# A token's two expert rows scattered to places of their own and summed by the next reader, with the padding written beside the last pass

## The chip, the core and the metric

The kernel runs on one core of a Trainium2 chip. The metric is the device time of one execution in microseconds; the median of several runs counts, and a profile shows one execution instruction by instruction. The core's engines work beside each other and meet at semaphores: TensorE (PE) multiplies and transposes, VectorE (DVE) and ScalarE (ACT) work elementwise, GpSimd (POOL) does small vector work and issues the indirect DMAs, SyncE (SP) issues most other DMAs in order. Sixteen DMA engines move the data.

## The reference

The input x holds 32 sequences of 256 tokens, 8192 rows of 128 float32 numbers. Four blocks follow each other, each on a layer norm of x:

```python
x = x + attention_a(layernorm(x))     # 16 heads of 8, softmax over the 256 tokens of a sequence, relative bias
x = x + ffn(layernorm(x))
x = x + attention_b(layernorm(x))     # the same token of all 32 sequences attends to each other
x = x + ffn(layernorm(x))

def ffn(x):                           # shared expert on every token, two of seven routed experts by a router
    out = expert(x, sg, su, sd)
    scores, idx = top_k(softmax(x @ wr.T + rb), 2)      # scores are then divided by their sum
    w = sum(scores[..., None] * one_hot(idx, 7), -2)
    for e in range(7):
        out = out + w[..., e:e + 1] * expert(x, rg[e], ru[e], rd[e])
    return out
# expert(h, g, u, d) = (silu(h @ g.T) * (h @ u.T)) @ d.T, inner width 352
```

## The kernel before

Half A computes attention A and the feed-forward behind it, half B does the same with attention B. Each half has two stages.

The passes. 16 passes of 512 tokens (4 tiles of 128 partitions) run as a software pipeline: the head of pass p+1 (load, norm, projections), the attention of pass p and the tail of pass p-1 (second norm, router, shared expert) are interleaved. The order of the steps on each engine is fixed ahead of time by a planner (`order`) from a table of costs (`WORK`) and of dependences (`needs_head`, `needs_attention`, `needs_tail`). The tail gives every token its rank in the list of each of its two experts (`rank`, VectorE, with the running counts in `taken`) and sends its normed row twice, to the two experts' regions of the DRAM tensor `sent`, by 8 indirect scatters of 128 rows (`scat`, L839, GpSimd). A row in `sent` is 130 words: 128 values, the routing share and the token's row number. The tail also stores x with attention and shared expert added: to `x2` in half A (L679), to `x3` in half B (L682). In half B the head loads x2 by four DMAs a pass (L653); GpSimd adds the output bias to a copy (`keep`, L812) and computes the roots of the norms (L790 to L800).

The expert stage (`blocks`). When all ranks are known, VectorE makes a table of 38 blocks of 512 rows (`make_table`, L1227): which expert, and which rows of `sent`. SyncE writes padding rows behind the end of each expert's list (`pad`, L684), fetches per block the weights (L708, L710, 3 buffers) and the rows (L698, 6 buffers), in the order weights of block b+3, rows of block b+6. The fetch of rows waits until the block six before has been added. TensorE turns the rows (L1324), makes gate and up products in three tiles (L1451 to L1453), the down product (L1526) and transposes back (L1536). VectorE weights the result with the share (`weigh`, L1278). GpSimd adds the 512 result rows into x2 or x3 by four indirect DMAs with addition (L850). Two rows of one token may lie in two blocks, so each block first waits for the adds of all blocks before it (L848):

```python
pool.wait_ge(emptied["T1"], use("E", b, "back"))
after(pool, added, 64 * b)
for t in range(TOK):
    pool.indirect_dma_start(out=dst[:, :], ..., in_=yo[:, b % 2, t, :], in_offset=None, compute_op=ALU.add)
```

Between the halves GpSimd clears the operand buffers `kw` (L858) and `vw` (L860 to L863) of attention B. At the end SyncE copies x3 to the output in four DMAs (L740).

## Time and profile before

| | us |
|---|---|
| median of 3 runs | 2653.86 (2653.19 to 2663.66) |
| the profiled execution | 2653.52 |
| its span from first to last instruction | 2651.7 |
| busy: TensorE, VectorE, ScalarE, GpSimd | 2083.7, 1596.5, 1165.9, 975.9 |
| passes of half A, about | 0 to 1130 |
| expert blocks of half A, about | 1151 to 1544 |
| passes of half B, about | 1562 to 2230 |
| expert blocks of half B, about | 2246 to 2637 |

A profile line names an engine, a line of the kernel and an operation, with tensors as output<-input. The chain of work that ended last is followed back from the last instruction: at each step to what released it. A share of busy time is an average over stages with different limits; what a change in one stage is worth is read in that stage. "issue" is time in which an engine waited for nothing that the profile shows, and SPq, POOLq stand for an engine's queue of DMA-issuing instructions. Landing is the time until a DMA's data has arrived and its semaphore tells so.

### The profile page before, as it was taken

Reading aid. Unit: us, or ns where it says so; the run is one execution under the profiler, and the core shown is the slowest. Engines: PE = TensorE matmul, PEld = TensorE weight load, DVE = VectorE, ACT = ScalarE, POOL = GpSimd, SP = SyncE. Lnnn points to the kernel's source line nnn. Section 1 sums busy time; section 2 is a strip of 40 time slices with the busy share of each in tenths; the row PEclk is TensorE's granted clock in tenths of the full one; section 3 lists DMA queues with packets and bytes.
Section 4 is the critical chain, followed back from the end, with each engine's and each line's share of the span. In section 5 each row is a group of like instructions: output and inputs, shape, how many; then the busy total and the mean of one; then the engine's idle time right before and its main releaser. Section 6 shows DMA issues by size and latency. Waiting matters only on the chain.

```text
span 2651.7 us, 42166 instructions
## 1 busy us (share of the span) xinstructions
PE 2083.7 (79%) x13346; PEld 1340.6 (51%) x13346; DVE 1596.5 (60%) x5677; ACT 1165.9 (44%) x2413; POOL 975.9 (37%) x1113
## 2 busy tenths in 40 slices
PE   6979797979898989858878737777777774988873
PEld 4646464656555555545555414544544443555552
DVE  4758585857676666745555426666666653655542
ACT  4949494849585858522223212322222231333321
POOL 1131414140312121326665653323343322566654
PEclk8979798979888888979999969888888886999986
DMA  5021212121111111066676511111110114566664
GB/s 169 18 77 61 77 61 77 56 83 46 59 47 55 50 49 45 23 144 149 149 153 137 122 24 33 31 29 39 37 37 25 31 28 118 128 153 152 150 141 107
DMA packets 193947, 210.31 MB, mean 79 GB/s; under 512 B 20944, under 2 KB 159440, under 8 KB 193664
## 3 DMA queue, kind: packets, MB, share of 16 engines
q1 hardware_dynamic: 139520, 161.09, 20.2%
q0 software_dynamic: 54208, 46.53, 10.6%
q8 instruction: 110, 1.80, 0.3%
q14 instruction: 109, 0.89, 0.1%
HBM read 114.03 MB, written 59.95 MB: 66 GB/s over the span
## 4 chain that ended last, share of the span: by engine, by line
PE 35%; POOL 19%; DVE 14%; DMA 11%; issue 11%; ACT 4%; another core or an unknown queue 4%; SPq 1%; POOLq 0%; DVEq 0%; ACTq 0%
POOL x L850 13%; DMA x<-arena 10%; PE bank_T L1387 8%; PE bank_S L1377 5%; PE bank_O L1400 4%; PE bank_E L1451 2%; PE bank_Y L1489 2%; DVE arena L1084 2%; DVE z L1097 2%; PE bank_E L1342 2%; POOL rs L792 2%; ACT z L914 2%; PE bank_E L1452 2%; PE bank_E L1453 2%
## 5 line engine op out<-in xcount | busy, mean ns | idle before, releaser
L850 POOL DMA_INDIRECT x<-arena x304 | 470.7, 1548 | 354.0 <-DMA x<-arena 179.6
L1097 DVE CUSTOM_DVE_ANT_0 z<-bank_S,arena 128x256 f32<-128x256 f32 x1024 | 377.6, 420 | 143.0 <-PE bank_S L1377 105.7
L839 POOL DMA_INDIRECT sent<-xs,target x256 | 253.5, 990 | 568.0 <-DVE target L1205 501.6
L914 ACT ACTIVATE z<-z,nm 128x256 f32<-128x256 f32 x1024 | 437.5, 500 | 29.8 <-DVE nm L1097 27.8
L922 ACT ACTIVATE probT<-bank_T 128x512 f32<-128x512 f32 x512 | 284.5, 588 | 120.9 <-remote 64.9
L1387 PE MATMUL bank_T<-cst,z 128*128 128x128 f32 x2048 | 320.7, 292 | 19.8 <-ACT probT L922 9.6
L1387 PEld LDWEIGHTS bank_T<-cst,z 128*128 128x128 f32 x2048 | 237.4, 148 | 112.8 <-issue 49.9
L790 POOL TENSOR_SCALAR rs<-moments 128x4 f32<-128x4 f32 x64 | 16.8, 262 | 675.6 <-DVE moments L1039 673.5
L1377 PE MATMUL bank_S<-arena_r 32*128 32x256 f32 x1024 | 202.3, 342 | 24.3 <-DVE nm L1097 23.3
L1377 PEld LDWEIGHTS bank_S<-arena_r 32*128 32x128 f32 x1024 | 122.5, 194 | 108.5 <-issue 70.4
L976 ACT ACTIVATE arena<-bank_E 128x512 f32<-128x512 f32 (+1 forms) x114 | 68.1, 598 | 193.4 <-PE bank_E L1453 190.0
L1400 PE MATMUL bank_O<-probT,arena 128*32 128x256 f32 x2048 | 148.8, 411 | 3.6 <-issue 2.5
L1265 DVE SCALAR_TENSOR_TENSOR arena<-arena,bank_E 128x512 f32<-128x512 f32 (+1 forms) x114 | 78.2, 686 | 120.8 <-ACT arena L976 117.0
L976 ACT ACTIVATE arena<-bank_S 128x512 f32<-128x512 f32 (+1 forms) x114 | 68.1, 597 | 185.9 <-PE bank_S L1453 177.6
L1451 PE MATMUL bank_E<-arena_r 128*128 128x512 f32 (+1 forms) x228 | 105.3, 462 | 55.7 <-issue 52.8
L1265 DVE SCALAR_TENSOR_TENSOR arena<-arena,bank_S 128x512 f32<-128x512 f32 (+1 forms) x114 | 78.2, 686 | 112.5 <-ACT arena L976 109.1
L1451 PE MATMUL bank_S<-arena_r 128*128 128x512 f32 (+1 forms) x228 | 104.3, 457 | 48.6 <-issue 48.6
L956 ACT ACTIVATE th<-bank_E 128x512 f32<-128x512 f32 (+1 forms) x96 | 57.0, 594 | 176.4 <-PE bank_E L1453 169.0
L1451 PE MATMUL bank_E<-xh,shared_hi 128*128 128x512 f32 (+1 forms) x192 | 99.4, 518 | 34.1 <-DVE th L1210 21.4
L1526 PE MATMUL bank_O<-arena 128*128 128x512 f32 (+1 forms) x228 | 121.9, 617 | 5.0 <-DVE arena L1275 5.0
L966 ACT ACTIVATE arena_r<-bank_T 128x512 fp32r<-128x512 f32 x76 | 45.5, 599 | 182.3 <-PE bank_T L1324 177.1
L1526 PE MATMUL bank_Y<-arena 128*128 128x512 f32 (+1 forms) x228 | 121.7, 616 | 0.0
(172 smaller groups left out, 4120.9 us busy)
## 6 DMA issues: line engine op xcount, KB each, us to landing
arena_r<-w_split SPq DMA_DIRECT2D x76, 704.0 KB
arena_r<-arena SPq DMA_DIRECT2D x128, 256.0 KB, 2.4
arena<-sent SPq DMA_DIRECT2D x76, 260.0 KB
arena<-in_wdp SPq DMA_DIRECT2D x76, 192.0 KB
x<-arena POOLq DMA_INDIRECT x304
xin<-in_x SPq DMA_DIRECT2D x16, 256.0 KB, 3.8
h<-in_x SPq DMA_DIRECT2D x16, 256.0 KB, 3.1
sent<-xs,target POOLq DMA_INDIRECT x256
```

What stands on the lines that cost most here:

```text
L839: pool.indirect_dma_start(out=sent[:, :], out_offset=bass.IndirectOffsetOnAxis(ap=target[:, s, k, t:t + 1].bitcast(U32), axis=0), in_=xs[: ...
L850: pool.indirect_dma_start(out=dst[:, :], out_offset=bass.IndirectOffsetOnAxis(ap=xr[:, b % ROW_RING, t, D + 1:RW].bitcast(U32), axis=0), i ...
L914: last = act.activation(zt, zt, ACT.Exp, bias=nm[:, u % NM_RING, t:t + 1], scale=-1.0)
L922: act.activation(probT[:, u % PT_RING, :], bank[f"T{n % 2}"][:, :], ACT.Copy).then_inc(emptied[f"T{n % 2}"], 1)
L976: act.activation(eth[0:size, k % 2, :], bank[e][0:size, :], ACT.Tanh, scale=0.5).then_inc(eth_ready, 1)
L1097: last = dve.tensor_tensor_reduce(z[:, u % Z_RING, t * SEQ:(t + 1) * SEQ], bank[s][:, t * SEQ:(t + 1) * SEQ], bias_a[:, h, P - P * t:P - P ...
L1265: dve.scalar_tensor_tensor(out=a, in0=a, scalar=1.0, in1=bank[e][0:size, :], op0=ALU.add, op1=ALU.mult).then_inc(emptied[e], 1)
L1377: last = pe.matmul(bank[name][:, t * SEQ:(t + 1) * SEQ], qx[own, s, 0, g, lo:lo + P].bitcast(F32R), qx[own, s, 1, g, b * SEQ:(b + 1) * SEQ ...
L1387: last = pe.transpose(bank[name][:, c:c + P], z[:, u % Z_RING, t * SEQ + k * P:t * SEQ + (k + 1) * P], ident)
L1400: last = pe.matmul(bank["O"][32 * j:32 * j + 32, 0:SEQ], vx[:, p % 2, 2 * b + k, c:c + 32], probT[:, u % PT_RING, k * SEQ:(k + 1) * SEQ], ...
L1451: pe.matmul(dst, high_w, high_x, start=True, stop=False)
L1526: last = pe.matmul(bank[y][:, :], w_d[0:size, b % WEIGHT_RING, i, :], ehid[0:size, b % 2, i, :], start=i == 0, stop=i == NT - 1)
```

## The change

The adds into x2 and x3 become plain scatters. Each token's two result rows go to places of their own in a new DRAM tensor `added_rows` of the half: the first at the token's row number, the second 8192 rows further. Padding rows carry numbers of their own behind those (13 tiles of 512). The wait for earlier blocks on GpSimd goes; the counter `added` is split in two by the block's parity (`wait_added`).

The next reader sums. In half B a pass loads, beside its x2 rows, the two sets of expert rows into `ya` (12 DMAs in place of 4), and GpSimd adds both into `xin` (step `join`) before the norm and `keep` read it. At the end x3 has been loaded to on-chip buffers (`pieces`) by eight DMAs issued among blocks 4 to 11 of half B; SyncE and ScalarE load the two sets of rows (`shares`, eight DMAs each), VectorE adds both to the pieces (`last_sums`) and SyncE stores each piece to the output.

The padding goes out earlier. After the rank of pass 14 VectorE copies `taken` to `ends` (step `pads`), and SyncE writes two chunks of padding rows from DRAM behind the end of each expert's list (14 DMAs); the scatters of the last pass wait for them. The padding tiles are made on GpSimd in passes 7 to 13 of half A. `make_table` loses its last cast and, in half B, its wait for the adds.

Between the halves `kw` is cleared once the last up product of the blocks is done, and `vw` is cleared on VectorE (`clear_values`). The planner's tables get the steps `join` and `pads` and a dearer `load`. Cut to its core:

```diff
 }
+WORK["A"]["pads"] = {"dve": 0.25, "sync": 6.5}
 WORK["B"] = {k: v for k, v in WORK["A"].items() if k not in ("cut", "scores", "probs", "mix", "context", "flip")} | {
-    "keep": {"pool": 1.3}, "turn1": {"pe": 0.6, "act": 2.06}, "v": {"pe": 1.0, "dve": 1.18}, "spr": {"sync": 10.7},
+    "load": {"sync": 5.4}, "join": {"pool": 2.7}, "keep": {"pool": 1.3}, "turn1": {"pe": 0.6, "act": 2.06}, "v": {"pe": 1.0, "dve": 1.18}, "spr": {"sync": 10.7},
     "scores": {"pe": 1.1, "dve": 1.3, "act": 0.6}, "probs": {"pe": 0.5, "act": 0.5},
...
     flip = z[:, 5, 0:P]
-    raw = sb("raw", [P, 2 * INNER])
-    raw_hi = sb("raw_hi", [P, 2 * INNER], F32R)
-    raw_lo = sb("raw_lo", [P, 2 * INNER], F32R)
+    spare = sb("spare", [P, 6 * INNER])
+    raw, raw_hi, raw_lo = (spare[:, 2 * INNER * k:2 * INNER * (k + 1)] for k in range(3))
...
+    ya = spare[:, 0:4 * CHUNK].rearrange("p (s k t d) -> p s k t d", s=2, k=2, t=TOK)
...
+    pieces = [z[:, 2 * c:2 * c + 2, :] for c in range(3)] + [probT[:, 2 * c:2 * c + 2, :] for c in range(4)] + [hid[:, 0:2, :]]
+    shares = [arena_r[:, 0:8192].rearrange("p (c r) -> p c r", c=8), arena[:, 0:8192].rearrange("p (c r) -> p c r", c=8)]
...
+    added_rows = [nc.dram_tensor(f"added_{k}", [2 * ROWS + (ROUTED + IDLE) * CHUNK, D], F32).ap() for k in range(2)]
+    pad_rows = nc.dram_tensor("pad_rows", [ROUTED, CHUNK, RW], F32).ap()
     sent = nc.dram_tensor("sent", [EXPERTS * CAP, RW], F32).ap()
...
                 if p == 0:
-                    sp.wait_ge(added, 64 * BLOCKS)
+                    for b in (BLOCKS - 2, BLOCKS - 1):
+                        wait_added(sp, b)
                 after(sp, kept, p - 1)
                 for j in range(4):
-                    sp.dma_start(xin[32 * j:32 * j + 32, s, :, :], positions(x2, p, j)).then_inc(x_landed[s], 16)
+                    own = slice(32 * j, 32 * j + 32)
+                    sp.dma_start(xin[own, s, :, :], positions(x2, p, j)).then_inc(x_landed[s], 16)
+                    for k in range(2):
+                        sp.dma_start(ya[own, s, k, :, :], positions(added_rows[0][k * ROWS:(k + 1) * ROWS, :], p, j)
+                                     ).then_inc(ya_landed[s], 16)
...
             def tail(kind, p, step, n):
+                if step == "pads":
+                    pad("AB".index(kind))
+                    return
                 sp.wait_ge(emptied["Y"], use(kind, p, "end"))
...
-                sp.wait_ge(table_ready, half + 1)
+                sp.wait_ge(ends_ready, half + 1)
+                for k in range(2):
+                    sp.wait_ge(pads_stored[k], 16 * ((ROUTED + IDLE + 1 - k) // 2))
                 for e in range(ROUTED):
-                    r = sp.value_load(table[0:1, 2 * BLOCKS + e:2 * BLOCKS + e + 1], min_val=0,
-                                      max_val=EXPERTS * CAP - CHUNK)
-                    sp.dma_start(sent[bass.ds(r, CHUNK), :].rearrange("(t p) c -> p t c", p=P), padding[:, :, :]
-                                 ).then_inc(padded, 16)
+                    r = sp.value_load(ends[0:1, e:e + 1], min_val=0, max_val=EXPERTS * CAP - 2 * CHUNK)
+                    for k in range(2):
+                        sp.dma_start(sent[bass.ds(r + k * CHUNK, CHUNK), :], pad_rows[e]).then_inc(padded, 16)
...
             def blocks(half):
-                pad(half)
+                sp.wait_ge(table_ready, half + 1)
                 first, last = half * BLOCKS, (half + 1) * BLOCKS
...
                     sp.wait_ge(stored[k], store_count("AB"[half], PASSES - 2 + k))
-                sp.wait_ge(padded, 16 * ROUTED * (half + 1))
-                sp.wait_ge(idle_padded, 16 * IDLE)
+                sp.wait_ge(padded, 16 * 2 * ROUTED * (half + 1))
                 for b in range(first, first + ROW_RING):
...
                         fetch_rows(b + ROW_RING)
+                    if half and first + 4 <= b < first + 12:
+                        c = b - first - 4
+                        sp.dma_start(pieces[c], rows_of(x3, c)).then_inc(piece_landed[c], 16)
...
             blocks(1)
-            sp.wait_ge(added, 64 * 2 * BLOCKS)
-            piece = ROWS // 4
-            for k in range(4):
-                sp.dma_start(out[k * piece:(k + 1) * piece, :], x3[k * piece:(k + 1) * piece, :]).then_inc(copied_out, 16)
-            sp.wait_ge(copied_out, 16 * 4)
+            for b in (2 * BLOCKS - 2, 2 * BLOCKS - 1):
+                wait_added(sp, b)
+            for c in range(8):
+                sp.dma_start(shares[0][:, c, :], rows_of(added_rows[1], c)).then_inc(share_landed[c], 16)
+            for c in range(8):
+                sp.wait_ge(ended_sum, c + 1)
+                sp.dma_start(rows_of(out, c), pieces[c]).then_inc(out_stored, 16)
+            sp.wait_ge(out_stored, 16 * 8)
...
+            def make_padding(j):
...
+                s = j % 2
+                if j < 2:
+                    pool.memset(padding[:, s, :, :], 0.0).then_inc(padding_ready, 1)
+                    pool.wait_ge(setup_landed, 4 * 16)
+                    pool.wait_ge(padding_ready, 2 * j + 1)
+                else:
+                    pool.wait_ge(pads_stored[s], 16 * (j // 2))
+                pool.tensor_scalar(padding[:, s, :, D + 1:RW].bitcast(I32), row_no[:, 2, :].unsqueeze(2),
+                                   ROWS + j * CHUNK, None, ALU.add).then_inc(padding_ready, 1)
+                pool.wait_ge(padding_ready, 2 * j + 2 if j < 2 else j + 3)
+                first = ROUTED * CAP + (j - ROUTED) * CHUNK
+                dst = pad_rows[j] if j < ROUTED else sent[first:first + CHUNK, :]
+                pool.dma_start(dst.rearrange("(t p) c -> p t c", p=P), padding[:, s, :, :]).then_inc(pads_stored[s], 16)
...
                     return
-                pool.wait_ge(x_landed[p % 2], x_count("B", p))
+                if step == "join":
+                    s = p % 2
+                    pool.wait_ge(x_landed[s], x_count("B", p))
+                    pool.wait_ge(ya_landed[s], 16 * 8 * (p // 2 + 1))
+                    pool.tensor_tensor(xin[:, s, :, :], xin[:, s, :, :], ya[:, s, 0, :, :], ALU.add).then_inc(join_step, 1)
+                    pool.wait_ge(join_step, p + 1)
+                    pool.tensor_tensor(xin[:, s, :, :], xin[:, s, :, :], ya[:, s, 1, :, :], ALU.add).then_inc(joined, 1)
+                    return
+                pool.wait_ge(joined, p + 1)
                 if p >= 3:
...
                         split(g + 1)
-                    elif g == ROUTED:
-                        make_padding()
+                    elif g < PASSES - 2:
+                        for j in range(2 * (g - ROUTED), min(2 * (g - ROUTED) + 2, ROUTED + IDLE)):
+                            make_padding(j)
                 elif step == "dup":
...
                     for k in range(2):
-                        step_rows = CHUNK * p if kind == "A" else 4 * TOK * p
+                        step_rows = k * ROWS + (CHUNK * p if kind == "A" else 4 * TOK * p)
                         pool.tensor_scalar(xs[:, s, k, :, D + 1:RW].bitcast(I32),
...
                     if n == 0:
+                        if p == PASSES - 1:
+                            pool.wait_ge(padded, 16 * 2 * ROUTED * ("AB".index(kind) + 1))
                         pool.wait_ge(ranked, g + 1)
...
             def blocks(half):
-                dst = (x2, x3)[half]
                 for b in range(half * BLOCKS, (half + 1) * BLOCKS):
                     pool.wait_ge(emptied["T1"], use("E", b, "back"))
-                    after(pool, added, 64 * b)
                     for t in range(TOK):
                         pool.indirect_dma_start(
-                            out=dst[:, :], out_offset=bass.IndirectOffsetOnAxis(
+                            out=added_rows[half][:, :], out_offset=bass.IndirectOffsetOnAxis(
                                 ap=xr[:, b % ROW_RING, t, D + 1:RW].bitcast(U32), axis=0),
-                            in_=yo[:, b % 2, t, :], in_offset=None, compute_op=ALU.add).then_inc(added, 16)
+                            in_=yo[:, b % 2, t, :], in_offset=None).then_inc(added[b % 2], 16)
...
             blocks(0)
-            pool.wait_ge(added, 64 * BLOCKS)
+            done = BLOCKS - 1
+            pool.wait_ge(filled[bank_of("E", done, "up", NT - 1)], use("E", done, "up", NT - 1))
             pool.memset(kw, 0.0).then_inc(kw_ready, 1)
-            pool.wait_ge(kw_ready, 1)
-            pool.memset(vw[:, :, :, :, :, :], 0.0).then_inc(vw_ready, 1)
-            for h in range(4):
-                pool.wait_ge(vw_ready, h + 1)
-                pool.memset(vw[32 * h:32 * h + 32, :, :, :, h, DH:VW], 1.0).then_inc(vw_ready, 1)
-            pool.wait_ge(vw_ready, 5)
             run("pool", "B", head, None, tail)
...
             blocks(1)
+            for b in (2 * BLOCKS - 2, 2 * BLOCKS - 1):
+                wait_added(act, b)
+            for c in range(8):
+                act.dma_start(shares[1][:, c, :], rows_of(added_rows[1][ROWS:, :], c)).then_inc(share_landed[c], 16)
...
                     route(kind, p, n)
+                elif step == "pads":
+                    settle()
+                    dve.tensor_copy(ends[:, :], taken[:, :]).then_inc(ends_ready, 1)
                 elif step == "rank":
+                    if p == PASSES - 1:
+                        dve.wait_ge(ends_ready, "AB".index(kind) + 1)
                     if p == 0:
...
             run("dve", "A", head, attention, tail)
+            def clear_values():
...
+                done = BLOCKS - 1
+                for b in (BLOCKS - 2, BLOCKS - 1):
+                    wait_added(dve, b)
+                dve.wait_ge(filled["T1"], use("E", done, "back"))
+                dve.memset(vw[:, :, :, :, :, :], 0.0).then_inc(vw_ready, 1)
+                for h in range(4):
+                    dve.wait_ge(vw_ready, h + 1)
+                    dve.memset(vw[32 * h:32 * h + 32, :, :, :, h, DH:VW], 1.0).then_inc(vw_ready, 1)
...
+            def last_sums():
+                for c in range(8):
+                    x = pieces[c].rearrange("p s t -> p (s t)")
+                    dve.wait_ge(piece_landed[c], 16)
+                    dve.wait_ge(share_landed[c], 32)
+                    dve.tensor_tensor(x, x, shares[0][:, c, :], ALU.add).then_inc(sum_step, 1)
+                    dve.wait_ge(sum_step, c + 1)
+                    dve.tensor_tensor(x, x, shares[1][:, c, :], ALU.add).then_inc(ended_sum, 1)
```

## Rows read from the trace of the kernel before

**Rows 1.** The page's part 4: shares of the chain by line.
```profile
POOL x L850 13%; DMA x<-arena 10%; PE bank_T L1387 8%; PE bank_S L1377 5%; PE bank_O L1400 4%; PE bank_E L1451 2%; PE bank_Y L1489 2%; DVE arena L1084 2%; DVE z L1097 2%; PE bank_E L1342 2%; POOL rs L792 2%; ACT z L914 2%; PE bank_E L1452 2%; PE bank_E L1453 2%
```

**Rows 2.** Windows of three stages: us, busy PE, PEld, DVE, ACT, POOL, PEclk, DMA share, GB/s.
```profile
1151.00:1544.00 393.00, 309.80 (x1216) 201.43 (x1216) 207.07 (x304) 109.46 (x190) 235.34 (x152) 0.93 0.62 132
2246.00:2637.00 391.00, 315.06 (x1216) 204.71 (x1216) 207.04 (x304) 109.45 (x190) 235.34 (x152) 0.91 0.62 133
1562.00:2230.00 668.00, 504.95 (x4448) 307.92 (x4448) 415.69 (x1466) 186.10 (x336) 227.49 (x376) 0.86 0.13 33
```

**Rows 3.** The chain in order of time, half A's blocks: start us, length us, what.
```profile
1170.31 1.61 POOL x L850
...
1175.94 3.23 DMA x<-arena
...
1341.48 3.27 DMA x<-arena
...
1351.04 3.28 DMA x<-arena
...
1540.78 3.20 DMA x<-arena
```

**Rows 4.** Timeline of TensorE, half A's blocks: start us, length us, operation [idle before <-releaser].
```profile
1151.85 1.11 PE L1324 MATMUL bank_T<-cst,arena 128*128 128x128 f32 x4 [28.15 <-DMA arena<-sent]
...
1163.17 0.80 PE L1451 MATMUL bank_S<-arena_r 128*128 128x512 f32 x1
...
1173.46 0.60 PE L1324 MATMUL bank_T<-cst,arena 128*128 128x128 f32 x4
...
1176.16 0.60 PE L1536 MATMUL bank_T<-cst,arena 128*128 128x128 f32 x4
...
1181.06 0.60 PE L1324 MATMUL bank_T<-cst,arena 128*128 128x128 f32 x4
...
1519.34 1.11 PE L1536 MATMUL bank_T<-cst,arena 128*128 128x128 f32 x4 [0.69 <-ACT arena L983]
```

**Rows 5.** Timeline, a weight issue and the products that waited for it.
```profile
1346.78 0.21 SPq L708 DMA_DIRECT2D arena_r<-w_split  x1
...
1352.47 0.47 PE L1451 MATMUL bank_S<-arena_r 128*128 128x512 f32 x1 [1.66 <-issue]
```

**Rows 6.** Timeline, a plain token scatter of the last pass of half A.
```profile
1127.48 0.96 POOL L839 DMA_INDIRECT sent<-xs,target  x1 [0.30 <-issue]
```

**Rows 7.** DMA view from 1145 to 1152 us: weight and row loads fill all engines.
```profile
DMA packets 2155, 2.56 MB, mean 365 GB/s; under 512 B 112, under 2 KB 1918, under 8 KB 2155
```

**Rows 8.** Timeline of VectorE and SyncE from the table to the first blocks.
```profile
1129.35 0.17 DVE L1253 CAST table<-taken 128x8 int32<-128x8 f32 x1
...
1130.55 7.27 SPq L690 DMA_DIRECT2D sent<-padding  x7
1138.59 0.38 SPq L708 DMA_DIRECT2D arena_r<-w_split  x1
...
1142.45 0.33 SPq L710 DMA_DIRECT2D arena<-in_wdp  x1
1145.41 6.51 SPq L698 DMA_DIRECT2D arena<-sent  x6
```

**Rows 9.** Timeline of the seam between the halves.
```profile
1556.53 2.48 POOL L812 TENSOR_TENSOR h<-xin,bc 128x512 f32<-128x512 f32 x2
...
1561.61 1.11 DVE L1044 TENSOR_SCALAR xn<-xin,moments,rs 128x128 f32<-128x128 f32 x4 [12.86 <-POOL rs L800]
...
1562.78 1.11 PE L1324 MATMUL bank_Y<-cst,xn 128*128 128x128 f32 x4 [42.33 <-DVE xn L1044]
...
1566.59 1.96 DVE L1044 TENSOR_SCALAR xn<-xin,moments,rs 128x128 f32<-128x128 f32 x4 [2.67 <-POOL rs L800]
```

**Rows 10.** Instructions of L653: ns least, median, most; first and last start us.
```profile
L653 SPq DMA_DIRECT2D xin<-x x64: 303/432/1364, 1544.1 to 2086.5; - x64
```

**Rows 11.** Timeline of SyncE, the last copy.
```profile
2636.53 2.52 SPq L740 DMA_DIRECT2D out_x<-x  x4
```

More of the change, by code:

```diff
@@ L116 @@
 HAND_OVER = 0.22
-LANDING = {"load": 3.5, "spr": 6.0, "store": 3.0}
+LANDING = {"load": 3.5, "spr": 6.0, "store": 3.0, "pads": 8.0}
 def head_uses(kind, p):
@@ L193, in needs_head @@
             + ([("pool", p - 2, "keep", 0)] if kind == "B" else [])
+    if step == "join":
+        return [("sync", p, "load", 0)]
     if step == "keep":
-        return [("sync", p, "load", 0), ("dve", p - 3, "end", 0)]
+        return [("pool", p, "join", 0), ("dve", p - 3, "end", 0)]
     if step == "norm1":
@@ L324, in needs_tail @@
         return [("dve", p, "end", 0)]
-HEAD_STEPS = ("load", "keep", "norm1", "root1", "turn1", "q", "k", "cut", "spr", "v")
+HEAD_STEPS = ("load", "join", "keep", "norm1", "root1", "turn1", "q", "k", "cut", "spr", "v")
 ATTENTION_STEPS = ("flip", "scores", "probs", "mix", "context", "bturn", "bout")
@@ L344, in order @@
         for step in WORK[kind]:
-            if step == "flip" and p:
+            if step == "flip" and p or step == "pads" and p < PASSES - 1:
                 continue
@@ L364, in passing @@
     def passing(w, t):
-        if w[0] == "sync" and w[2] in ("load", "spr", "store"):
+        if w[0] == "sync":
             return LANDING[w[2]]
@@ L482, in program @@
     which = sb("which", [P, 2, BLOCKS])
-    table = sb("table", [P, 2 * BLOCKS + 8], I32)
+    table = sb("table", [P, 2 * BLOCKS], I32)
+    ends = sb("ends", [P, 8], I32)
     arena = sb("arena", [P, 10560])
@@ L1251, in make_table @@
                 then(dve.tensor_copy(table[:, 0:BLOCKS], which[:, 1, :]))
[L1252 to L1253 removed]
+                dve.tensor_copy(table[:, BLOCKS:2 * BLOCKS], which[:, 0, :]).then_inc(table_ready, 1)
             def low(b):
```

57 lines of the change are left out of this document (29 added, 28 removed).

## The prediction, made before the changed kernel was run

> **What bounds the kernel now.** I read the chain of work that ended last by line, then the windows of the stages, then the chain piece by piece inside a block stage, then TensorE's timeline there. The chain's largest items are the scatter-adds of L850 and their landing [rows 1]. They rule only the two expert stages, from 1151 to 1544 us and from 2246 to 2637 us; TensorE is busy for 310 of 393 and 315 of 391 us there [rows 2]. Piece by piece the chain there is a loop on GpSimd: four scatter-adds, the landing of the fourth 3.27 us after its start, and only then the next block's first, because L848 waits for every earlier block's adds. One turn takes 9.56 us (1341.48 to 1351.04); over 38 blocks, from the first landing piece at 1175.94 to the last at 1540.78, the mean is 364.84 / 37 = 9.86 us [rows 3]: stalls add 37 x 0.30 = 11 us.
>
> TensorE could go faster. In the first blocks, before the loop has caught up, a block's turn follows the one before after 7.60 us (1173.46 to 1181.06) [rows 4]. Later it waits at the head of each block (1.66 us at 1352.47) for weights that were issued at 1346.78 [rows 5]: SyncE sends them in order behind the row fetch, and that waits for the adds of an earlier block, landed at 1344.75 [rows 3]. At the end TensorE starts its last transposes at 1519.34, 24.6 us before the last add has landed at 1544.0 [rows 3, 4].
>
> **Part 1, plain scatters: the period of a block.** The wait of L848 goes and the scatter becomes plain. The nearest row is a token scatter of L839, the same operation with 520-byte rows: 0.96 us and a gap of 0.30, so 1.26 us each [rows 6], against 1.85 for an add with its gap. GpSimd then needs 4 x 1.26 = 5.0 us a block; at the adds' spacing 7.4. Both lie under 7.60. The DMA engines' share is 0.62 [rows 2], 6.1 us a block; a plain write reads no destination, so it doesn't grow, and 6.1 is under 7.60 too.
>
> What is late next? TensorE itself, if the weights' loop permits. A block's first scatter starts 7.1 us after the next block's products begin (1163.17 to 1170.31) [rows 3, 4]. The landing of a plain scatter lies between its own 0.96 us and the adds' 3.27 us after its start; I take 2.5, nearer the add because both write DRAM rows. All landed: 7.1 + 3 x 1.26 + 2.5 = 13.4 us. From landing to the products that the next weights feed it is 7.7 us now (1344.75 to 1352.47) [rows 3, 5]. So block b+4 may start 21.1 us after block b+1, and three blocks of 7.60 are 22.8: 1.7 us to spare. With adds' prices it would be 7.1 + 5.6 + 3.3 + 7.7 = 23.7, a period of 7.9. So I take TensorE's 7.60.
>
> The stage's length: first turn at 1151.85 to block 3's turn at 1173.46 is 21.6; 34 more periods 258.4; from the last turn to the back transposes beside it 2.7 (1173.46 to 1176.16), two more blocks 15.2, transposes 1.1 [rows 4]; then weighting and hand-over 1.2, scatters 3.8, landing 2.5. Sum 306.5. I keep half of the stalls (6 us), as those on GpSimd alone are mostly absorbed. Now it is 1544.0 - 1151.85 = 392.2. First half: 312.5 - 392.2 = -80. The second half takes 390.5 us until the copy at 2636.53 [rows 11] and gets eight 512 KB loads of x3 beside blocks 4 to 11, some 1.4 us of DMA each at 365 GB/s [rows 7], within the 1.7 us to spare; I add 2: -76. Splitting the counter over two semaphores costs nothing.
>
> **Part 2, the padding moved.** Now the table is ready at 1129.5, seven pad stores keep SyncE until 1137.8, weights go out from 1138.6 to 1142.8, rows at 1145.41 when the pads have landed, and TensorE starts 6.4 us later [rows 4, 8]. Without the pads the weights go out from about 1129.7 to 1133.9 and rows at 1134.2. The engines then owe 2.75 MB of weights and 0.27 MB of first rows; at 365 GB/s [rows 7] from 1131 that ends at 1139.3, with completion 1140.5. Gain 11 us in half A, and 10 in half B, where the rows repeat the pattern.
> The pads themselves, now 14 stores, stand in SyncE's queue after the rank of pass 14, ahead of stores of x2 or x3. Seven register loads with a store took 7.3 us [rows 8]; seven more stores at 0.43 [rows 10] make it about 11. They land about when the last pass's scatters, which now wait for them, would start anyhow. Behind that wait on GpSimd there are only those scatters, and their landing is needed by 1134. Price 0; if the landing slips by 8 us, 3 to 5 us each half. The 13 padding tiles made on GpSimd (a tiny addition and a DMA issue each, bounded by 13 x 1.26 = 16 us from [rows 6]) lie in attention passes ruled by other engines: 0.
>
> **Part 3, the seam between halves.** The last add has landed at 1544.0 [rows 3]. GpSimd then clears kw and vw, makes two biased copies and the root; TensorE starts at 1562.78, 18.8 us later [rows 9]. After: kw is cleared right behind the last scatters' issue and vw on VectorE, both done before they are needed; but SyncE sends 12 loads in place of 4 at 0.43 us [rows 10], 5.2 us, then 2.5 of landing, two joins of 1.24, statistics 1.3 (an estimate by the 1.11 of the normalising), root 2.6, normalise 1.1 [rows 9]: 15.2 us. That is -3.6; pass 1's load is later by the same eight issues, so I take -2.
>
> **Part 4, the join in the passes of half B.** Each of 16 passes gains eight load issues on SyncE (8 x 0.43 = 3.5 us) and two additions on GpSimd (2.5 us). Cover: loads are issued a pass ahead, and GpSimd is busy 227 of 668 us there [rows 2, 9, 10]. Queued behind the load on SyncE are the key spread and a store; behind the join on GpSimd roots and token scatters. A gain is excluded, since nothing is removed. Bounds: 0, and all exposed, 16 x (3.5 + 2.5) = 96 us. I take 0.4 us a pass, 6 us, because of the cover.
> VectorE may be slowed beside GpSimd: four normalising instructions take 1.96 us beside a biased copy and 1.11 without [rows 9]. At 0.85 us for each addition this would be 1.7 us a pass, 27 us if VectorE were always last; it is busy 416 of 668 us [rows 2], so a part lies in the 6 us and the rest in the range. The Trainium skill, GPSIMD Engine Reference, section Key points, says that GpSimd shares its SBUF interfaces with VectorE and contends with VectorE instructions in a 2-port mode or with two SBUF inputs; by that rule, which the trace bears out in the place named, the join is not free even where GpSimd has time.
>
> **Part 5, the end.** Now: the copy is issued at 2636.53 [rows 11] and the span ends at 2651.7, 15.2 us. After: two shares of 4.19 MB are read, added to x3's pieces by 16 VectorE instructions, and 4.19 MB are written: 12.6 MB at the 365 GB/s of weight and row loads [rows 7] is 34.5 us, with 1.7 for start and completion 36.2. The additions, by the normalising's 1.11 us for 512 elements [rows 9] at most 16 x 2.2 = 35 us, run beside it. So +21. Bounds: +14 if reads and writes overlap better, +30 if the writes of the last pieces trail.
>
> **Sum.** -80 - 76 - 11 - 10 - 2 + 6 + 21 = -152. The profiled execution took 2653.5 us (span 2651.7), within 0.4 us of the median of the runs. Forecast 2502 us, -5.7%.
>
> **Rivals.**
> (a) The join is not covered. SyncE works in order, so eight more issues delay the key spread, and roots queue behind joins. For it: VectorE and TensorE wait for roots at the seam already [rows 9]. Against: the loads go out a pass ahead. Half exposed it gives 48 in place of 6: about 2545.
> (b) The change doesn't free the expert stage: if weights or landing need 1.7 us more, the loop is level with TensorE, and each further microsecond adds a third of one to each of some 70 blocks. At 3 us beyond that, 70 us: 2572. Against it: the plain scatter's lighter row.
> (c) All is covered, the stalls vanish and the end overlaps: 2502 - 6 - 12 - 7 = 2477.
> (d) Slower: load, join and VectorE's slowing stand in series in every B pass, because the next pass's head waits for them. Place: the head of a pass; price 3.5 + 2.5 landing + 2.5 + 1.7 = 10.2 us, 11 with hand-overs: 16 x 11 = 176, less the 6 counted: 2672. It decides from 9.9 us a pass on, where 16 passes eat 152 + 6 us. Against it is that the load is issued a pass ahead.
>
> **How the numbers follow.** Chances: forecast 0.60, (a) 0.20, (b) 0.06, (c) 0.12, (d) 0.02. The likeliest gives 2502. The range 2472 to 2552 takes in (c), (a) and the end's bounds; (b), (d) and what lies further out are left to the other 2 in 10. About 0.5% (13 us) can be told from no change: faster 0.97, within 0.01, slower 0.02.
>
> **What would show it.** Expert stages: turns 7.6 us apart, no scatter that waits for a landing, TensorE at the top of the chain, a stage of about 312 us. The first block starts some 11 us after the table. TensorE's first turn of half B comes about 16 us after the last landing. From there to the first expert block of half B it is 683 us now [rows 2, 9]; 679 is expected, and 720 would mean (a). From the last landing to the end 36 us. The forecast is wrong if turns stay above 8 us, if half B's passes grow by over 30 us, or if the end takes over 50.

## The result, and the profile after

The changed kernel takes 2560.66 us in the median of five runs (2545.97 to 2562.34), the kernel before 2653.19 beside it: a ratio of 0.964, 95% interval [0.961, 0.966]. It is faster by 3.6%; 5.7% was forecast, and the time lies 9 us above the upper end of the range. The profiled execution is the fastest of the five: 2545.97 us, 107.5 less than the profiled execution before. By stages, both profiles read at the same events:

| Stage | before | after | gain | forecast |
|---|---|---|---|---|
| start to first block turn of half A | 1151.9 | 1142.3 | -9.6 | -11 |
| first turn to last landing, half A | 392.2 | 313.9 | -78.3 | -80 |
| seam, to TensorE's first turn of half B | 18.8 | 18.1 | -0.7 | -2 |
| passes of half B, to the first block turn | 683.3 | 719.1 | +35.8 | -4 (+6 join, -10 pads) |
| expert blocks of half B, to the end part | 390.5 | 317.2 | -73.3 | -76 |
| end | 15.2 | 33.5 | +18.3 | +21 |

Five of six rows lie within 3 us of the forecast. One failed, by 40 us, and it is nearly the whole miss of 44 us between the two profiled executions.

The windows of the three stages after, against [rows 2] (columns: window and its length, then busy time with the number of instructions of PE, PEld, DVE, ACT, POOL, the granted clock as a share of 2.4 GHz, DMA share, GB/s):

```profile
1142.00:1456.00 314.00, 295.91 (x1216) 196.72 (x1216) 207.06 (x304) 109.42 (x190) 147.06 (x153) 0.98 0.54 164
1474.00:2193.00 719.00, 531.91 (x4448) 329.44 (x4448) 426.11 (x1464) 187.01 (x336) 262.85 (x404) 0.81 0.19 50
2193.00:2510.00 317.00, 298.54 (x1216) 198.97 (x1216) 207.10 (x304) 109.42 (x190) 145.88 (x152) 0.97 0.57 177
```

TensorE is now busy for 296 of 314 us in the expert stage (310 of 393 before). In the passes of half B it is the other way: 532 us busy in 719, at a granted clock of 0.81 in place of 0.86 (the clock is given as a share of 2.4 GHz, the higher of its two levels; the lower is 1.2 GHz).

TensorE's timeline at the head of the expert stage, and GpSimd's, after (start, length, engine, line and operation, in brackets the idle time ahead of it and what ended it); they answer to [rows 3, 4, 6]:

```profile
1142.27 1.12 PE L1402 MATMUL bank_T<-cst,arena 128*128 128x128 f32 x4 [18.73 <-DMA arena<-sent]
...
1147.52 1.06 PE L1402 MATMUL bank_T<-cst,arena 128*128 128x128 f32 x4
1155.55 0.60 PE L1402 MATMUL bank_T<-cst,arena 128*128 128x128 f32 x4
1163.14 0.60 PE L1402 MATMUL bank_T<-cst,arena 128*128 128x128 f32 x4
...
1182.64 0.96 POOL L903 DMA_INDIRECT added<-arena  x1 [2.85 <-DVE arena L1338]
1183.90 0.96 POOL L903 DMA_INDIRECT added<-arena  x1 [0.30 <-issue]
```

Most turns are 7.60 to 7.66 us apart (23 of the 37 distances in half A; 13 are 7.9 to 9.4, as the 8.03 shown here), and GpSimd waits for VectorE's weighting, no longer for a landing.

What half B's passes did is seen where VectorE ends a pass (the tile xo). First the kernel before, then the changed one:

```profile
1735.68 0.68 DVE L1224 TENSOR_TENSOR xo<-bank_Y,h 128x512 f32<-128x512 f32 x1
1791.07 0.68 DVE L1224 TENSOR_TENSOR xo<-bank_Y,h 128x512 f32<-128x512 f32 x1
1817.50 0.68 DVE L1224 TENSOR_TENSOR xo<-bank_Y,h 128x512 f32<-128x512 f32 x1
```

```profile
1704.75 0.68 DVE L1283 TENSOR_TENSOR xo<-bank_Y,h 128x512 f32<-128x512 f32 x1
1750.39 0.69 DVE L1283 TENSOR_TENSOR xo<-bank_Y,h 128x512 f32<-128x512 f32 x1 [0.34 <-PE bank_Y L1573]
1795.10 0.68 DVE L1283 TENSOR_TENSOR xo<-bank_Y,h 128x512 f32<-128x512 f32 x1
```

Before, passes ended in pairs: 55.4 us, then 26.4, 82 for two. After, they end evenly, 45.6 and 44.7, 90 for two. A delay inside each pass would stretch the pairs; this is another order of steps. The diff has its source: the planner's table was told a dearer `load` (5.4 us) and the new `join` (2.7), and from them it wrote half B's order anew on every engine but SyncE.

### The profile page after: what moved, and what is told of

Same layout as the page of the kernel before. It is cut to its first block, busy times and chain, and to the rows that moved or that the text cites. A ratio compares the mean times of both kernels' runs of the same rounds, so it can differ in the third digit from the quotient of the medians.

```text
span 2544.1 us, 42386 instructions
## 1 busy us (share of the span) xinstructions
PE 2075.5 (82%) x13346; PEld 1349.1 (53%) x13346; DVE 1635.0 (64%) x5698; ACT 1167.4 (46%) x2413; POOL 842.1 (33%) x1160
## 3 DMA queue, kind: packets, MB, share of 16 engines
q10 hardware_dynamic: 1152, 4.19, 0.4%
## 4 chain that ended last, share of the span: by engine, by line
PE 60%; DVE 13%; issue 8%; POOL 6%; another core or an unknown queue 5%; ACT 4%; SPq 2%; DMA 2%; DVEq 0%; POOLq 0%; ACTq 0%
PE bank_T L1465 8%; PE bank_S L1455 5%; PE bank_E L1529 4%; PE bank_O L1478 4%; PE bank_Y L1604 4%; PE bank_O L1604 4%; PE bank_E L1531 4%; PE bank_E L1530 4%; PE bank_S L1494 3%; PE bank_Y L1567 3%; PE bank_S L1529 2%; DVE z L1151 2%; PE bank_S L1530 2%; PE bank_S L1531 2%
## 5 line engine op out<-in xcount | busy, mean ns | idle before, releaser
L962 ACT ACTIVATE z<-z,nm 128x256 f32<-128x256 f32 x1024 | 437.4, 500 | 29.2 <-DVE nm L1151 26.5
L903 POOL DMA_INDIRECT added<-arena x304 | 291.7, 960 | 362.0 <-DVE arena L1338 287.3
L1478 PE MATMUL bank_O<-probT,arena 128*32 128x256 f32 x2048 | 149.9, 414 | 3.7 <-issue 2.9
L1529 PE MATMUL bank_E<-xh,shared_hi 128*128 128x512 f32 (+1 forms) x192 | 105.5, 550 | 40.9 <-DVE th L1269 24.8
L1567 PE MATMUL bank_Y<-hid,shared_d 128*128 128x512 f32 (+1 forms) x192 | 120.8, 742 | 4.3 <-DVE taken L1260 3.1
```

Of the source, the lines that this page charges most:

```text
L903: pool.indirect_dma_start(out=added_rows[half][:, :], out_offset=bass.IndirectOffsetOnAxis(ap=xr[:, b % ROW_RING, t, D + 1:RW].bitcast(U32 ...
L962: last = act.activation(zt, zt, ACT.Exp, bias=nm[:, u % NM_RING, t:t + 1], scale=-1.0)
L1478: last = pe.matmul(bank["O"][32 * j:32 * j + 32, 0:SEQ], vx[:, p % 2, 2 * b + k, c:c + 32], probT[:, u % PT_RING, k * SEQ:(k + 1) * SEQ], ...
L1529: pe.matmul(dst, high_w, high_x, start=True, stop=False)
L1567: last = pe.matmul(bank["Y"][:, :], shared_d[0:size, n, :], hid[0:size, n, :], start=n == 0, stop=n == NT - 1)
```

## The experiments

The diffs show what each run changes in the changed kernel, or in the kernel before where the text says so; "..." marks what is left out. In all of them the passes are measured from the end of pass 1 to the end of pass 15 (xo to xo, "passes 1 to 15"), and the head from the first load of half B to the end of pass 1. All results stand in one table behind the texts.

**The old order with the new work.** The planner plans half B without `join`, `pads` and the dearer `load`; then both steps are put in.

```diff
-    "load": {"sync": 5.4}, "join": {"pool": 2.7}, "keep": {"pool": 1.3}, ...
+    "keep": {"pool": 1.3}, ...
...
+put(dve_lane, (LAST, "pads", 0), dve_lane.index((LAST - 1, "rank", 0)) + 1)
+put(sync_lane, (LAST, "pads", 0), sync_lane.index((LAST, "spr", 0)) + 1)
+for p in range(PASSES):
+    put(pool_lane, (p, "join", 0), pool_lane.index((p, "keep", 0)) - (p == 3))
```

> The changed kernel whole, but with half B's steps on every engine in the order of the kernel before; the join stands directly ahead of its biased copy (pass 3: one step earlier) and the pads behind the same neighbours as in the changed kernel. From TensorE's first turn of half B to the first expert block it is 683 us in the kernel before and 719 us in the changed kernel. Theory of the order (the planner, told of a load of 5.4 us and a join of 2.7, put the passes in another order, and that costs the time): about 680 us, the run near 2505. Theory of the work (the eight loads and two additions themselves cost it, whatever the order): 719 or more, the run at 2545 to 2560 or slower; by the planner's own costs this order with the new work would be 86 us longer than the order it chose, so 800 us would say that the new order was a rescue.

Measured: 571.3 us for passes 1 to 15 (605 and 615 with the new order), and the run at 2523.75, 26 us under the changed kernel beside it. The old order is the better one on the chip, and the planner's own estimate (86 us longer) had the wrong sign. It does not give all back: the stage of the table above takes 695.0 us, where about 680 was expected, and the head is 125.9 us where it was 112.1 before.

**The new order without the work**, and with the loads alone.

```diff
-                    for k in range(2):
-                        sp.dma_start(ya[own, s, k, :, :], ...).then_inc(ya_landed[s], 16)
...
-                    pool.tensor_tensor(xin[:, s, :, :], xin[:, s, :, :], ya[:, s, 0, :, :], ALU.add)...
-                    pool.tensor_tensor(xin[:, s, :, :], xin[:, s, :, :], ya[:, s, 1, :, :], ALU.add)...
+                    pool.memset(tick[:, :], 0.0).then_inc(joined, 1)
```

> The changed kernel with its new order of half B, but half B doesn't read the expert rows of half A and doesn't add them (eight loads and two additions a pass are left out, a tiny memset on GpSimd stands for the join). Theory of the order: the passes still take 705 to 719 us, the run at 2530 to 2560. Theory of the work: about 673 us (683 less the 10 us of the moved padding), the run near 2500.

> As the run without loads and sums, but the eight loads a pass are made; only GpSimd's two additions are left out. If SyncE's issues or the traffic cost the time, the passes take over 705 us where the run without both is at 673; if GpSimd's additions cost it (in time of their own or by slowing VectorE), both runs are near 673; by the theory of the order all three lie at 705 to 719.

Measured: 613.9 us with neither loads nor sums, 604.6 with the loads alone; by the stage of the table above 727.7 and 718.1, where the work would have given about 673 and the order 705 to 719. Taking the work out gives nothing back in the passes; only the head shrinks, by 6 to 8 us.

**The changed kernel once more**, unchanged.

> The changed kernel once more, for the spread: its five times lay between 2546 and 2562 us and the profiled one was the fastest. If the spread sits in half B's passes, their 719 us differ by up to 15 us in this profile and the granted clock there with them; if not, they stay within 3 us.

Measured: 2549.96 us in the median, its profile at 2567.5. The spread sits in two places: passes 1 to 15 took 614.8 us (604.7 in the first profile), and half A's passes, the same code, put the first row load at 1143.8 us (1135.1). Over ten profiles with the same attention in half A that load starts between 1125.5 and 1150.8 us.

**The new order alone, in the kernel before.**

```diff
-ORDERS = {kind: order(kind) for kind in "AB"}
+ORDERS = {kind: {e: [x for x in lane if x[1] not in ("join", "pads")] for e, lane in order(kind).items()} for kind in "AB"}
```

(with the planner's tables of the changed kernel above it)

> The kernel before with one thing changed: half B's steps stand on every engine in the order of the changed kernel (its joins and pads taken out of the lanes); scatter-adds, padding, loads and end are those of the kernel before. Theory of the order: passes 1 to 15 of half B go from 563 us to 605 to 615, the granted clock there from 0.86 to about 0.80, and the run from 2654 to about 2700. If the new order costs only together with the changed kernel's pads or plain scatters, they stay at 563 to 575 and the run at 2654.

Measured: 614.5 us for passes 1 to 15 in place of 563.1, the run at 2710.06 against 2660.54, ratio 1.017 [1.009, 1.025]. The order alone costs 50 us in a kernel that has no join at all.

**One suspect within the order.** VectorE's reciprocal L1184, which needs a mix from TensorE, waits 103 us in passes 1 to 15, up to 7.5 us at a time. The profile puts 32 us of it to the mix and names no releaser on this core for the other 71; the theory is that the mix stands behind a down product.

```diff
...
+for p in range(3, 12):
+    if p + 2 < PASSES:
+        behind("pe", "turn1", p + 2, "mix", TOK - 1, p + 1)
+    behind("pe", "end", p, "mix", TOK - 1)
+    behind("pe", "down", p, "mix", TOK - 1)
+    behind("act", "sum", p, "probs", TOK - 1)
+    behind("dve", "end", p, "mix", TOK - 1)
```

> The changed kernel with its new order, but for passes 3 to 11 TensorE's down product, which the new order puts between the mixes of the next pass's attention (6.down between 7.mix and 7.mix), goes behind the last mix, with the steps that hang on it (the sum on ScalarE, the end on VectorE, the next turn). The first to the last output row tile of half B's passes 1 to 15 (xo to xo) takes 605 and 615 us in two profiles of the changed kernel, 571 with the old order. Theory of the queue (VectorE waits up to 7.5 us a pass, 103.7 us in all at L1184, for a mix that stands behind a down product): these nine passes get back 3 to 5 us each, so 570 to 585. Theory of the clock (the order as a whole leaves TensorE at a granted clock of 0.80 in place of 0.86, wherever the product stands): 600 or more and a clock still near 0.80.

(`behind` takes the steps named out of an engine's order and puts them behind the last mix.) Measured: 656.4 us, 42 to 52 more. The theory of the queue falls. TensorE idles 175 us in place of 150, so between the mixes the product seems to have filled a time in which TensorE otherwise waits for them.

**Another order by the planner**, with TensorE's steps costed as recorded.

```diff
...
+    "mix": {"pe": 0.7, "dve": 0.5}, "bturn": {"pe": 0.8, "act": 0.5}, "bout": {"pe": 1.9, "dve": 0.6},
...
+for step, pe in (("q", 1.5), ("k", 1.5), ("turn2", 0.8), ("logits", 1.9), ("rank", 1.6), ("gate", 1.2), ("up", 1.2),
+                 ("down", 1.7), ("end", 0.8)):
+    WORK["B"][step] = WORK["B"][step] | {"pe": pe}
```

> The changed kernel with load and join planned as there (5.4 and 2.7 us), but TensorE's steps of half B costed as the trace records them (a query product 1.5 us in place of 0.95, a down product 1.7 in place of 0.9, the mix 0.7 in place of 1.8, and so on), so that the planner writes another order. If the planner went wrong because its TensorE was too fast, passes 1 to 15 take 575 us or less; if its order is a matter of chance as far as the chip goes, 590 to 620.

Measured: 582.5 us, between both theories' numbers. In these passes truer costs give a better order than the changed kernel's, but not as good a one as the old. The head takes 127.4 us in place of 114 to 116, and the run as a whole can't be told from the changed kernel's: 0.958 [0.955, 0.961] of the kernel before, against 0.960 [0.954, 0.965].

| Kernel | order of half B | run, median | head | passes 1 to 15 | TensorE busy | idle | clock |
|---|---|---|---|---|---|---|---|
| before | old | 2653.2 | 112.1 | 563.1 | 434.4 | 128.7 | 0.86 |
| old order, new work | old | 2523.8 | 125.9 | 571.3 | 433.6 | 137.7 | 0.86 |
| the same, new head | old | 2516.3 | 112.9 | 577.1 | 436.8 | 140.3 | 0.85 |
| the same, side by side | old | 2507.0 | 110.7 | 570.1 | 438.2 | 131.9 | 0.85 |
| TensorE's costs | third | 2545.3 | 127.4 | 582.5 | 440.3 | 142.2 | 0.84 |
| after | new | 2560.7 | 114.3 | 604.7 | 454.8 | 149.9 | 0.81 |
| after, once more | new | 2550.0 | 115.9 | 614.8 | 464.2 | 150.6 | 0.79 |
| no loads, no sums | new | 2542.7 | 108.4 | 613.9 | 466.2 | 147.7 | 0.78 |
| loads, no sums | new | 2534.1 | 108.3 | 604.6 | 457.3 | 147.3 | 0.81 |
| before, new order | new | 2710.1 | 110.1 | 614.5 | 464.1 | 150.4 | 0.79 |
| after, wait put back (below) | new | 2608.1 | 114.0 | 611.6 | 463.2 | 148.4 | 0.79 |
| down behind | new, moved | 2584.1 | 115.1 | 656.4 | 481.4 | 175.0 | 0.78 |

The column of the order sorts the passes, the work doesn't. Every kernel with the new order, with and without join, idles 147 to 151 us; what differs between 604 and 615 is TensorE's busy time, longer at the lower clock. The windows behind four of the rows, first of the kernel before and of the kernel before with the new order:

```profile
1656.00:2219.00 563.00, 434.34 (x3840) 264.46 (x3836) 349.67 (x1233) 159.36 (x288) 196.70 (x323) 0.86 0.12 32
```

```profile
1658.00:2273.00 615.00, 464.29 (x3820) 290.15 (x3812) 353.58 (x1230) 158.02 (x285) 193.75 (x324) 0.79 0.11 30
```

then of the changed kernel without the work, and of the old order with it:

```profile
1576.00:2190.00 614.00, 465.85 (x3800) 288.82 (x3789) 354.41 (x1230) 158.39 (x285) 191.55 (x331) 0.78 0.14 35
```

```profile
1586.00:2157.00 571.00, 433.29 (x3839) 267.97 (x3836) 350.16 (x1234) 158.56 (x288) 223.92 (x346) 0.86 0.18 48
```

Nearly the same number of matmuls takes 464 us in one order and 434 in the other. So of the 51 us that the order costs in the kernel before, 30 are TensorE's instructions, longer at a lower clock, and some 21 are idle time (matmul ends are modelled, so the split is rough). Windows of 7 us of the changed kernel show what stood ahead of a low clock:

```profile
1781.00:1788.00 7.00, 5.33 (x112) 3.03 (x111) 2.52 (x12) 2.31 (x4) 4.01 (x4) 1.00 0.09 31
1788.00:1795.00 7.00, 0.84 (x5) 0.42 (x4) 0.36 (x2) 0.00 (x0) 3.83 (x4) 0.71 0.14 48
1795.00:1802.00 7.00, 6.76 (x22) 4.78 (x23) 2.73 (x11) 3.37 (x7) 0.66 (x2) 0.56 0.18 37
...
1851.00:1858.00 7.00, 4.20 (x15) 3.58 (x16) 6.37 (x31) 0.60 (x1) 3.46 (x6) 0.60 0.26 65
1858.00:1865.00 7.00, 6.78 (x22) 2.92 (x24) 4.75 (x17) 1.29 (x3) 0.80 (x4) 0.50 0.22 62
```

and with the old order:

```profile
1858.00:1865.00 7.00, 2.55 (x21) 0.85 (x20) 4.17 (x18) 0.00 (x0) 2.29 (x7) 0.97 0.43 117
1865.00:1872.00 7.00, 6.26 (x63) 2.50 (x62) 6.75 (x12) 3.70 (x7) 0.75 (x3) 0.79 0.01 2
1872.00:1879.00 7.00, 6.89 (x127) 5.28 (x127) 4.77 (x12) 3.14 (x6) 0.00 (x0) 1.00 0.00 0
```

In the changed kernel TensorE was busy for 0.84 of 7 us; then 6.76 us of work ran at 0.56, that is, mostly at 1.2 GHz. The old order has such stalls too (2.55 of 7 us), but fewer and shorter: in this pair of passes 4 of 12 windows lie at 0.80 or less, against 6 of 13 here. The Trainium skill, TensorE: Matmul & The Clock Gate, section HAM oscillation, describes a loop of products broken up by waits for DMA: its work runs in part at the lower clock, and the loss comes on top of the waits. The windows here agree, with waits of other kinds. Whether the clock or the stalls come first was not separated; both come with the order.

**Is the gain of the expert stage the kind of the scatter, or the wait?** Plain scatters, but with the wait for the block ahead put back.

```diff
                     pool.wait_ge(emptied["T1"], use("E", b, "back"))
+                    if b:
+                        wait_added(pool, b - 1)
```

> The changed kernel with plain scatters, but each block's scatters wait again until those of the block ahead have landed. If the gain of the expert stages (392 to 314 us from the first turn to the last landing) lies in the lighter scatter, it stays: the loop on GpSimd is then 3 x 1.26 + 2.3 of landing + 0.3 = 6.4 us, under TensorE's 7.60, and the stage stays at 314 to 320 us. If it lies in the wait that went, the stage goes back towards 392: at a landing as late as an add's (3.27 us) plus the hand-over the loop would be 7.4 us, so over 350 us would mean that more than that loop waits for the landing.

Measured: from the first row load to the first load of half B 349.0 us, where it is 398.6 before and 321.0 after; by the stage of the table above 345.5, between the two theories. So the lighter scatter gives 50 of the 78 us while the wait stands, and then the missing wait 28; a plain scatter's landing of 2.3 us, as expected there, would have left the wait nothing. Pieces of the chain of waits (start, length, what):

```profile
1303.49 0.96 POOL added L905
...
1307.28 4.15 DMA added<-arena
...
1316.25 3.88 DMA added<-arena
...
1324.66 5.11 DMA added<-arena
...
1472.25 2.23 DMA added<-arena
```

The fourth plain scatter of a block lands 4.10 us after its start in the mean of 36 blocks, later than a fourth add (3.39 in the mean of 38 before, of which [rows 3] has some): 4.33 us in the mean of the first 32 (2.6 to 5.9), 2.2 in each of the last four. The loop is 3 x 1.26 + 4.10 + 0.7 = 8.6 us, above TensorE's 7.60. Adds without the wait were not tried: two of them may meet in one row.

**The head of half B.** With the old order VectorE waits for the statistics of pass 2, and so for a load, ahead of the first values.

```diff
+for step in [(1, "join", 0), (1, "keep", 0)]:
+    pool_lane.remove(step)
+    put(pool_lane, step, pool_lane.index((1, "root1", 0)))
+for n in range(NORM):
+    dve_lane.remove((2, "norm1", n))
+    put(dve_lane, (2, "norm1", n), dve_lane.index((1, "v", 0)))
```

> The kernel with the old order of half B (passes 1 to 15: 571 us, but 126 us from the first load to the end of pass 1, against 114 and 116 in the changed kernel and 112 in the kernel before), and with two swaps at its head taken from the new order: GpSimd takes the root of pass 0 ahead of the join of pass 1, VectorE the first values ahead of the statistics of pass 2, which wait for a load. If the head's loss is that the old order waits there for joins that it did not have, 114 to 116 us and 10 to 12 us off the run: near 2513. If it is SyncE's issues, it stays at 126.

Measured: head 112.9 us (125.9), a little under the 114 to 116 expected; passes 1 to 15 took 577.1. The run is at 2516.31, 0.947 [0.943, 0.951] of the kernel before, which can't be told from the 0.952 [0.946, 0.957] of the old order alone.

**A token's two rows side by side in DRAM.**

```diff
-        return np.concatenate([a, b, ROWS + a], 1)
+        return np.concatenate([2 * a, 2 * b, ROWS + a], 1)
...
-                        step_rows = k * ROWS + (CHUNK * p if kind == "A" else 4 * TOK * p)
+                        step_rows = k + 2 * (CHUNK * p if kind == "A" else 4 * TOK * p)
...
+                    sp.dma_start(ya[own, s, :, :, :].rearrange("p t k d -> p t (k d)"), both[j][p]).then_inc(ya_landed[s], 16)
```

> The kernel with the old order and the new head, and a token's two expert rows side by side in DRAM, so that both come in one load of 1 KB pieces: four load issues a pass for them in place of eight, and the last sums read both rows as one piece. SyncE saves 4 x 0.46 = 1.9 us a pass. If its issues count only where a load is waited for, the head gains 4 to 6 us and passes 1 to 15 nothing, the run 5 us under the one without this; if they delay the key spread in every pass, passes 1 to 15 gain 8 us or more as well. The transfers of the last sums may gain up to 5 us, or lose that if the strided additions on VectorE (1.23 us each now) grow past 1.5 us.

Measured: 2506.99 us, ratio to the kernel before 0.944 [0.939, 0.949], against 0.960 [0.954, 0.965] of the changed kernel once more: it beats both. Against the kernel without this step (0.947 [0.943, 0.951]) the gain is not clear of the noise. The head gains 2.2 us, not 4 to 6. The stretch from the first row load of half B to the end goes from 357.4 to 351.8, but 5 us of that lie ahead of the last scatter, in the expert blocks, and from the last scatter to the end it is 35.5 us for 36.1: the last sums gain next to nothing. Passes 1 to 15 take 570.1 us, but the old order had 571.3 with eight loads too, so nothing there can be put down to SyncE's issues.

## Why the prediction failed, step by step

**Part 4, the join in the passes, is the step that failed.** It priced the join at 6 us "because of the cover", on the order of steps that the rows of before showed. Measured in the profile: +44 (from 683.3 to 719.1 it is 35.8, and the moved padding had given back 8.5 in the same stretch; the second profile of the changed kernel has 730.1 us there). The cover was there: without loads and sums, the passes are as long. What was missed stood in the diff: `load` at 5.4 and `join` at 2.7 in `WORK["B"]` go into the planner, and the rows of [rows 2] belonged to an order that would no longer exist. With the old order kept, load and join cost 8 us in passes 1 to 15 (563.1 to 571.3) and 14 at the head; with two swaps at the head 14 and 1. So in that order the work costs 15 to 22 us, where 6 were forecast (one profile each; the three of that order have 570 to 577 us in passes 1 to 15). In the new order it costs nothing in passes 1 to 15 and 6 to 8 us at the head; there the miss is the order.

**Rival (a)** named the right number (719 where "720 would mean (a)", 2546 in the profiled run against 2545) for a wrong reason. It holds SyncE's eight issues and GpSimd's joins to be the cause; both were taken out and nothing came back in the passes, and with the old order kept they cost 15 to 22 us, not the 48 of the rival. That the number fits is luck. A length alone could not tell the two apart, so it was a weak sign to name.

**Part 1** came out at -78.3 and -73.3 for -80 and -76. Its landing term of 2.5 us was mis-sized. With the wait put back it measured 4.10 us. In the changed kernel itself SyncE's next row fetch, which stood waiting for that landing in 28 of 32 blocks, goes out 5.32 us after the start of the fourth scatter in the mean of the 32, where it was 4.07 before. By its own sum, with 4.10, the weights' loop would then be 22.7 us of the 22.8 that three blocks give, so the 1.7 us to spare were all but used up. The trace shows it: most turns held at 7.60, but 13 of 37 were late. In the two places shown TensorE stands ahead of the first product with new weights; the weights of the first went out at 1185.44, behind the row fetch of 1184.27:

```profile
1185.44 0.34 SPq L744 DMA_DIRECT2D arena_r<-w_split  x1
...
1192.21 0.47 PE L1529 MATMUL bank_E<-arena_r 128*128 128x512 f32 x1 [0.71 <-issue]
...
1201.64 0.47 PE L1529 MATMUL bank_S<-arena_r 128*128 128x512 f32 x1 [1.58 <-issue]
```

From the first turn to the last turn it took 291.0 us for a forecast of 286, and from there to the last landing 22.9 for 26.5. So the stage's 313.9 for 312.5 is in part two misses against each other.

**Part 2** was right where it can be read by itself: the first turn came 13.3 us after the table (1129.0 to 1142.3), 22.5 before [rows 4, 8], and in half B the same stretch lost 8.5 us for 10. That the whole row of the table shows -9.6 too is luck, since the passes ahead of it move by up to 25 us between executions of the same code. SyncE took 15.7 us for the 14 pad stores, not 11, and the last pass's scatters waited 5.9 us for them, where the prediction put nothing:

```profile
1101.15 15.71 SPq L727 DMA_DIRECT2D sent<-pad_rows  x14
...
1119.76 0.96 POOL L894 DMA_INDIRECT sent<-xs,target  x1 [5.85 <-DMA sent<-pad_rows]
...
1128.99 0.18 DVE L1309 CAST table<-which 128x38 int32<-128x38 f32 x1
```

**Part 3** gave -0.7 for -2. VectorE and GpSimd at the seam, after:

```profile
1469.97 4.20 DVE L1096 TENSOR_SCALAR xn<-xin,moments,rs 128x128 f32<-128x128 f32 x4 [2.62 <-POOL rs L844]
...
1469.88 1.26 POOL L857 TENSOR_TENSOR xin<-xin,spare 128x512 f32<-128x512 f32 x1
1471.22 1.26 POOL L859 TENSOR_TENSOR xin<-xin,spare 128x512 f32<-128x512 f32 x1
1472.56 1.26 POOL L864 TENSOR_TENSOR h<-xin,bc 128x512 f32<-128x512 f32 x1
```

and in the run with the loads but without the sums:

```profile
1454.64 1.11 DVE L1095 TENSOR_SCALAR xn<-xin,moments,rs 128x128 f32<-128x128 f32 x4 [2.63 <-POOL rs L845]
```

The normalising of pass 0 was priced at 1.1 us and took 4.20 beside the second pass's two additions and biased copy. Part 4 had the price of such a neighbour, 0.85 us, and part 3 did not use it: three of them come to 2.6 of the 3.1 us.

**Part 5** gave 33.5 us for 36.2, with SyncE and ScalarE loading side by side and SyncE's stores beside the sums:

```profile
2510.60 4.18 SPq L778 DMA_DIRECT2D arena_r<-added  x8
2510.61 4.23 ACTq L1055 DMA_DIRECT2D arena<-added  x8
2518.60 5.59 SPq L781 DMA_DIRECT2D out_x<-z  x3
2526.41 8.01 SPq L781 DMA_DIRECT2D out_x<-probT  x4
2536.64 0.33 SPq L781 DMA_DIRECT2D out_x<-hid  x1
```

**The range** had a second flaw. It took the profiled execution for the median, which held for the kernel before; of the changed kernel the profiled execution is 15 us faster than the median and lies inside the range. The chances of what the range takes in (0.60, 0.20 and 0.12) also come to more than the 8 in 10 that it was meant to hold. The passes of either half move by 10 to 25 us from one execution to the next with the granted clock, while half A's expert stage stayed within 8 us (316 to 324). The clock of 720 to 920 us, in the same code, was 0.91 in one profile and 0.81 in another.

**What stays open** is which of the moved steps makes the new order slow. The one that was moved back made it slower.

## What to carry to other kernels

Where an order is planned from a table of costs, a change of the table can reorder every engine, and the rows of the old trace are no cover for the new order: keep the old order, put the new steps into it, and measure both. To tell a new step's cost from its order's, take the step's work out and leave its place. Here the stages in which TensorE stalls between short pieces of work were also those whose time spread; in the windows shown stalls were followed by work at the lower clock.

## What was not expected of the hardware

- The last of four plain scatters of 128 rows each lands later after its own start than the last of four accumulating ones while weights are loaded beside it: 4.33 us in the mean of 32 (2.6 to 5.9) with the wait put back, against 3.39 before; with no loads left it is 2.2. The plain ones also follow each other faster (1.26 us apart, not 1.85), so by the means (4.10 and 3.39) all four are down 7.9 us after the first one's start, against 8.9. Whether a single plain scatter is the slower one was not separated.
- Four normalising instructions on VectorE take 4.20 us beside three GpSimd instructions that each read two on-chip tensors (two additions and a biased copy), 1.96 beside one such copy [rows 9] and 1.11 alone. The Trainium skill, GPSIMD Engine Reference, section Key points, says that the two engines share their SBUF interfaces and contend when VectorE's instruction is in a 2-port mode or has two SBUF inputs; the trace agrees that they contend and gives the size, nearly a factor of four.
- The order of nearly the same instructions moves TensorE's granted clock over 560 to 615 us from 0.86 to 0.79.
